# A graph layer on one core: three stages that were programs of their own become one program, with a semaphore where drains stood

## What is computed

```
xn = layernorm(x)
agg = segment_sum(edge_attr, dst) / max(count, 1)           # scatter-add over the edges
h   = relu(concat(xn, agg) @ W1 + b1)                       # 1024 hidden
gnn = xn + h @ W2 + b2
mix = flow_attention(xn) @ W_out.T + b_out                  # sigmoid q and k, per token 8x8 over the heads
x1  = x + gnn + mix
x1n = layernorm(x1)
p   = softmax(mean(x1n, tokens) @ Wg + bg);  e = argmax(p)  # one expert for all tokens
out = x1 + p[e] * (x1n @ We[e] + be[e])
```

## Time and profile before

| | us |
|---|---|
| median of 3 runs | 2229.93 (2226.78 to 2238.92) |
| the profiled execution, its own time | 2234.79 |
| its span, first to last instruction | 2233.1 |
| PE busy in it | 1920.9 |
| mean granted clock of PE | 0.903 of full speed |

### The profile page before, as it was taken

How to read it: one execution, slowest core, us unless ns; L and a number is a source line. 1 busy time by engine, 2 the same in 40 slices (tenths; PEclk the granted TensorE clock), 3 DMA queues, 4 the chain that set the end, 5 groups by cost and what they waited for, 6 DMA issues and landing times. The chain is left out here.

```text
span 2233.1 us, 31150 instructions
## 1 busy us (share of the span) xinstructions
PE 1920.9 (86%) x10775; PEld 1522.4 (68%) x10775; DVE 1222.2 (55%) x3855; ACT 560.4 (25%) x1314; POOL 1341.5 (60%) x876
## 2 busy tenths in 40 slices
PE   2899999999999999688758877777855999998698
PEld 1688887788888788344347766666644888886586
DVE  3534435434344432477565655565536888884575
ACT  2322233322232222111122112111212333332210
POOL 3688888888888888777688878878850000000100
PEclk9899999999999999666867789898777999999799
DMA  9878777787787777887999999999856766652784
GB/s 270 191 154 152 142 139 150 149 153 151 133 160 141 136 142 125 230 206 166 268 228 176 183 189 163 182 202 160 151 98 197 228 207 209 200 180 97 264 303 146
DMA packets 516664, 397.45 MB, mean 178 GB/s; under 512 B 348027, under 2 KB 385163, under 8 KB 516510
## 3 DMA queue, kind: packets, MB, share of 16 engines
q1 hardware_dynamic: 387758, 340.83, 54.5%
q0 software_dynamic: 126640, 54.59, 24.0%
q10 hardware_dynamic: 2112, 0.07, 0.1%
HBM read 242.42 MB, written 152.96 MB: 177 GB/s over the span
## 5 line engine op out<-in xcount | busy, mean ns | idle before, releaser
L286 POOL DMA_INDIRECT table<-edge_sums,edge_row x831 | 1310.8, 1577 | 341.0 <-issue 253.7
L230 DVE SCALAR_TENSOR_TENSOR edge_sel<-edge_dst_all,edge_dst_f,upper 128x128 f32<-128x128 int16 x831 | 316.9, 437 | 105.0 <-PE edge_sum L242 104.8
L338 PE MATMUL pr_out_bank<-pr_norm_xT_hi,pr_w_hi 128*128 128x512 f32 (+1 forms) x832 | 330.1, 397 | 0.0
L338 PE MATMUL pr_out_bank<-pr_norm_xT_lo,pr_w_hi 128*128 128x512 f32 (+1 forms) x832 | 321.1, 386 | 0.0
L338 PE MATMUL pr_out_bank<-pr_norm_xT_hi,pr_w_lo 128*128 128x512 f32 (+1 forms) x832 | 320.9, 386 | 0.0
L242 PEld LDWEIGHTS edge_sum<-edge_attr,edge_sel 128*128 128x128 f32 x1662 | 230.6, 210 | 131.8 <-DVE edge_sel L230 106.5
L242 PE MATMUL edge_sum<-edge_attr,edge_sel 128*128 128x65 f32 x1662 | 244.9, 296 | 80.0 <-DVE edge_sel L230 79.7
L252 ACT ACTIVATE edge_sums<-edge_sum 128x260 f32<-128x260 f32 (+1 forms) x209 | 80.5, 386 | 578.0 <-PE edge_sum L242 546.1
L338 PEld LDWEIGHTS pr_out_bank<-pr_norm_xT_lo,pr_w_hi 128*128 128x128 f32 x832 | 156.8, 188 | 33.8
L338 PEld LDWEIGHTS pr_out_bank<-pr_norm_xT_hi,pr_w_lo 128*128 128x128 f32 x832 | 157.3, 189 | 29.5
L338 PEld LDWEIGHTS pr_out_bank<-pr_norm_xT_hi,pr_w_hi 128*128 128x128 f32 x832 | 157.2, 189 | 28.9
(11 more groups left out here) (202 smaller groups left out, 3254.2 us busy)
## 6 DMA issues: line engine op xcount, KB each, us to landing
edge_dst_all<-dst SPq DMA_DIRECT2D x103, 256.0 KB
edge_attr<-in_edge_attr SPq DMA_DIRECT2D x103, 256.0 KB
qk_T<-pr_stage SPq DMA_DIRECT2D x48, 512.0 KB, 3.3
h_pre_T<-pr_stage SPq DMA_DIRECT2D x48, 512.0 KB, 3.4
gn_pre<-h_pre_T SPq DMA_DIRECT2D x12, 2048.0 KB, 9.6
done<-qk_T SPq DMA_DIRECT2D x16, 1024.0 KB, 6.7
table<-edge_sums,edge_row POOLq DMA_INDIRECT x831
pr_norm_x<-in_x SPq DMA_DIRECT2D x12, 1024.0 KB, 8.6
```

Source lines behind the costliest of these rows:

```text
L230: op = dve.scalar_tensor_tensor(out=self.sel[q][0:rows, j, 0:rows], in0=self.dst_all[k][0:rows, t:t + m * (rows - 1) + 1:m], scalar=self.d ...
L286: pool.indirect_dma_start(self.c.table[t], bass.IndirectOffsetOnAxis(ap=self.row[k][0:rows, j:j + 1], axis=0), self.sums[k][0:rows, j, :], ...
L338: mm = pe.matmul(out, a, c, start=first and i == 0, stop=last and i == n - 1)
```

## The change

- The three programs from projection to expert become one. Their barriers and drains go. Engines go from stage to stage by themselves, held by semaphores.
- POOL: after the last scatter it waits for attention's stores of `base_rows` to land (`over`), then clears the 74 semaphores, waits for the scatters to land, and raises `front_done`. SP, ACT and DVE wait for `front_done` before the MLP's first block. SP no longer waits for the stores.
- SP loads the MLP's weights (2.5 MB, L315) before attention's tail block, behind the last full block's mixing. ACT and DVE split them from there on; DVE splits the W1 part before `front_done`, the two halves of W2 behind it.
- First MLP block: `hid` has four buffers for two; DVE adds two columns ahead of `low`; PE multiplies by W2 column by column as the lo parts come, in place of all after the last. `pre` of block 0, `base` of block 0 and `pre` of block 1 are loaded in that order.
- x1 is kept and stored in quarters of 128 rows, each store waiting for the landing of the one two before it. Before, one store of 512 rows per block.
- Expert: the gate starts on `parts_added`; x1n of block 0 is loaded when the MLP's last full block is through; every chunk of weights has its own semaphore, on which ACT, DVE and PE go; SP waits for the four chunks, not for the bias; the loops over blocks are written out; `out` has two semaphores for its stores, and DVE waits for them itself.

The diff, cut to its core:

```diff
@@ attend_stage
             for batch in batches[2:]:
                 edges.load_ahead(sp, *batch)
+            if b == NB - 1:
+                me.preload(sp)
             sp.wait_ge(acc_free, b * CH + len(subtiles(n)))
...
-        for k in range(2):
-            sp.wait_ge(stored[k], 16 * len(range(k, NB, 2)))
...
+    def over(eng):
+        eng.wait_ge(acc_free, FULL * CH + 1)
+        for k in range(2):
+            eng.wait_ge(stored[k], 16 * len(range(k, NB, 2)))
@@ gnn_stage
+    def preload(sp):
+        sp.wait_ge(before.mixed, FULL * before.STEPS)
+        weights.load(sp)
...
+        sp.wait_ge(c.front_done, 1)
         load_tables(0, BT)
-        weights.load(sp)
         sp.dma_start(b1[:, :], c.b1).then_inc(b1_in, 16)
         load_pre(0, 0, BT)
+        load_base(0, 0, BT)
         load_pre(1, 1, BT)
...
         turn_agg(0, BT)
-        weights.wait(pe)
-        for j in range(JH):
-            hidden(0, 0, BT, j)
-        output(0, 0, BT, 0)
+        weights.wait(pe, 2)
+        for j in range(BANKS):
+            hidden(0, 0, BT, j)
+        for j in range(JH):
+            if j + BANKS < JH:
+                hidden(0, 0, BT, j + BANKS)
+            if j == 0:
+                weights.wait(pe, 4)
+                pe.wait_ge(x1_ready, 1)
+            pe.wait_ge(h_ready, j + 1 + HIDS)
+            mm = products(pe, acc[0][:, :], [(h_hi[0][:, j, 0:P], h_lo[0][:, j, 0:P])],
+                          [(w2_hi[:, j, :], w2_lo[:, j, :])], first=j == 0, last=j == JH - 1)
+        mm.then_inc(acc_mm, 1)
         turn_agg(1, BT)
...
+        def store_x1(b, n, s):
+            r = subtiles(n)[s]
+            pool.wait_ge(x1_ready, b * CH + (AHEAD + s + 1))
+            if b or s >= 2:
+                pool.wait_ge(x1_stored[s % 2], b * 32 + s // 2 * 16)
+            pool.dma_start(c.x1[bass.ds(b * BT + s * P, r), :], x1[s][0:r, :]).then_inc(x1_stored[s % 2], 16)
@@ expert_stage
-            load_xT(0, 0, BT)
-            sp.wait_ge(gathered, 16 * (CH + 1))
+        sp.wait_ge(before.x1nT_stored[0], 16)
+        sp.wait_ge(before.hid_ready, before.AHEAD + FULL * JH)
+        sp.wait_ge(before.x1_ready, before.AHEAD + FULL * CH)
+        load_xT(0, 0, BT)
+        sp.wait_ge(gate_step, 13)
...
+        for ch in range(CH):
+            sp.wait_ge(gathered[ch], 16)
         load_x1(0, 0, BT)
...
         for ch in range(CH):
-            act.wait_ge(gathered, 16 * (CH + 1))
+            act.wait_ge(gathered[ch], 16)
             act.activation(w_hi[:, ch, :], w_raw[:, ch, :], ACT.Copy).then_inc(w_hi_ready, 1)
...
+        dve.wait_ge(before.parts_added, FULL * CH + 2)
@@ kernel_body, gpsimd
             edges.scatter_all(pool)
+            attend.over(pool)
             for sem in project.sems + norms.sems + scale.sems + edges.sems:
                 pool.sem_clear(sem)
             edges.finish_pool(pool)
+            pool.sem_inc(c.front_done, 1)
+            for stage in (gnn, expert):
+                stage.pool(pool)
```

More of the change, by code:

```diff
@@ L1206, in sem @@
         def sem(what):
[L1207 removed]
+            return c.whole.enter_context(nc.semaphore(f"at_{what}"))
         GROUPS = BT // GT
@@ L1211, in attend_stage @@
         HALF = P // 2
-        near = [[sb(f"near0_{half}", [P, 4, P]) for half in range(2)]]
+        near = [[sb(f"near{g}_{half}", [P, 4, P]) for half in range(2)] for g in range(2)]
         q, kk, v, x = [[sb(f"{what}0", shape)] for what, shape in
@@ L1633, in front_stages, with gnn_stage @@
         attend = attend_stage(nc, c, edges, scale)
[L1634 to L1663, removed]
-            edges.finish_pool(pool)
-def gnn_stage(nc, c):
+    return edges, [project, norms, scale, attend]
+def gnn_stage(nc, c, before):
+    me = Shared()
     with ExitStack() as ctx:
@@ new lines, in pe_program, with body @@
+    def pe_program(pe):
+        pe.wait_ge(c.gate_in, 32)
+        pe.wait_ge(gate_step, 1)
+        for ch in range(CH):
+            mm = pe.matmul(small[0:1, 0:EXPERTS], mean[:, ch:ch + 1], c.gate_w[:, ch, :], start=ch == 0,
+                           stop=ch == CH - 1)
+        mm.then_inc(gate_mm, 1)
+        pe.wait_ge(gate_step, 10)
+        pe.matmul(wide[:, 0:2], c.ones_row[:, :], pick[:, :], start=True, stop=True).then_inc(gate_mm, 1)
+        def body(b, k, n, after):
+            pe.wait_ge(xT_ready, b + 1)
+            for s, r in enumerate(subtiles(n)):
+                cut = slice(s * P, s * P + r)
+                if b or s:
+                    pe.wait_ge(y_ready, b * CH + s + 1)
+                for ch in range(CH):
+                    if b == 0 and s == 0:
+                        pe.wait_ge(w_ready, ch + 1)
+                    mm = products(pe, y_bank[s % BANKS][0:r, :], [(xT_hi[k][:, ch, cut], xT_lo[k][:, ch, cut])],
+                                  [(w_hi[:, ch, :], w_lo[:, ch, :])], first=ch == 0, last=ch == CH - 1)
+                mm.then_inc(y_mm, 1)
+        all_blocks(pe, U, body)
@@ new lines, in act_program, with high, ahead @@
+    def act_program(act):
+        def high(b, k, n):
+            act.wait_ge(x_in[k], landed(b, k, U))
+            act.activation(xT_hi[k][:, :, 0:n], xT[k][:, :, 0:n], ACT.Copy).then_inc(xT_hi_ready, 1)
+        act.wait_ge(gate_step, 3)
+        act.activation(prob_e[:, :], logit[:, :], ACT.Exp, bias=neg_top[:, :], accum_out=total[:, :]
+                       ).then_inc(gate_exp, 1)
+        high(0, 0, BT)
+        for ch in range(CH):
+            act.wait_ge(gathered[ch], 16)
+            act.activation(w_hi[:, ch, :], w_raw[:, ch, :], ACT.Copy).then_inc(w_hi_ready, 1)
+        high(1, 1, BT)
+        def ahead(b, k, n, after):
+            if later_size(b, 2):
+                act.wait_ge(y_mm, b * CH)
+                high(b + 2, (k + 2) % U, later_size(b, 2))
+        all_blocks(act, U, ahead)
```

893 lines of the change are left out of this document (446 added, 447 removed).

## The result

| | before | after |
|---|---|---|
| median (range), us | 2233.68 (2226.78 to 2238.92, 4 runs) | 2206.12 (2203.09 to 2208.45, 4 runs) |
| profiled execution, its own time / its span | 2234.79 / 2233.1 | 2203.09 / 2201.3 |

The ratio is 0.9878, 95% interval 0.9854 to 0.9903: 1.2% faster. The fourth run of before was taken beside the new kernel; with it the median of before is 3.75 us above the one that the prediction started from.

What follows compares the result with a forecast made beforehand. The prediction took PE's near-idle time in two junctions, around the MLP, to bound the kernel; 13.8 + 10.1 = 23.9 us less gave 2206.0 us against the median 2229.93, with a range from 2197 to 2215.

Steps and rivals of the forecast that it cites:

- the two junctions: Attention to MLP and MLP to expert stage, where PE stands nearly idle: 13.8 and 10.1 us to be won.
- the gate: Between attention and MLP: drain gone, but clears exposed and tail's store late, so tables are asked for 2.1 us later.
- the two chains: First MLP block, mean to add base, 15.9 us shorter; expert stage's loads, up to DVE's second bias addition, 10.1 us earlier.
- Steady parts gain nothing: MLP's steady part and expert stage: PE is busy throughout at full clock, so nothing can be gained there.
- The store's delay: Tail's store of base_rows, behind the weight loads on its queue: 2.0 us late, bounds 0 and 7.
- Rival 1: Attention to MLP: weights keep the tail's store back by 7 us, scatters suffer too; gain 17, time 2213 us; chance 12%.
- The first block: First MLP block: from the mean to add base 22.6 us in place of 38.5, so 15.9 us won.
- The clock fell at block 1's turn: MLP's second block: up to 2 us less gain if PE's clock falls in its 4 us wait there.
- The second junction: MLP to expert stage: the chain of loads ends last and moves by 10.1 us; PE waits about 4 us.
- The weights' bound: MLP to expert stage: the chain of expert weights alone would allow 14.0 us in place of 10.1.
- Quarter stores: MLP's x1 stores become the bound: each us of landing above 14 costs 2 us in 11 blocks; 2250 at 16; chance 5%.

Runs made afterwards that it cites:

- e4: The kernel before, with only the MLP's buffers allocated in the order of the changed kernel; 2222.13 us in a single run.
- e7: The changed kernel, but in the first MLP block PE multiplies by W2 only behind the last hidden column; 2215.03 us in a single run.
- e10: The changed kernel with the tail's store of base_rows issued as two transfers, of 96 and 10 rows, in place of one of 106; 2198.52 us.
- e5: The changed kernel, but SP loads x1 of block 0 and blocks 1 and 2 without waiting for the four gathers; 2200.65 us in a single run.
- e3: The changed kernel with POOL's clears ahead of its wait for the stores and the MLP's weight loads behind the tail's store; 2197.81 us, ratio to before 0.9857.
- e6: The changed kernel, but ACT splits no expert weights before all four gathers and the bias have landed; 2205.29 us in a single run.
- e12: The kernel before, with only w2_hi and w2_lo allocated behind part, lo ahead of hi; 2230.41 us in a single run.

## Why the prediction was right, point by point

- **The time.** 2206.0 predicted, 2206.12 measured. The mechanism of the two junctions was right, but that the last digit agrees is luck: 3.9 us too little gain (5.0 missed in the MLP, 3.1 too few taken off at the gate, 2.0 more in the two chains than I had), and a median of before that was 3.75 us too low, cancelled.
- **Steady parts gain nothing: the step that failed outright.** I wrote that in the MLP's steady part nothing could be gained because PE is busy for all of it at full clock. I had shown only that nothing makes PE *wait*. The change also moved the buffers, which my list of the change leaves out; two of the three kinds of products became some 2% shorter, and with 0.48 us in each block that is the 5.0 us (e4, with nothing but the buffers moved: 5.4).
- **The gate: right direction, mis-sized.** The clears took 5.6 us behind the store's landing, as said. The store's delay was 5.0, not 2.0: the weights ended 1.8 us later than I had worked out (13.5 us behind the full store's issue, not 11.7), and the tail's store was issued 6.9 us behind the full one in this run, not 8.3. Rival 1 priced this case at 7 us; the truth lies between, inside the bounds. (Its sum of 17 does not follow from that: 23.9 less the 4.9 us between 7 and 2.1 is 19.0; the scatters' share in it has no row.) With another end of attention the term would have come out nearly right: in e7 the tail's store was issued 9.9 us behind the full one and landed in 7.7, 1.1 late. The store's own 4 us at 50 GB/s I took for given, though my text had it on 2 of 16 engines and so how to shorten it: e10.
- **The first block: right.** 22.6 us from the mean to `add base`, 21.8 measured; `low` at 1.3 us a column (1.26), with 0.7 us lost to PE in two of them where I had 1.1; DVE's sum of the next tables ends last. `pre` was in time. The clock fell at block 1's turn, which I had as a bound; that it would fall again in the expert stage I had not.
- **The second junction: right, in place and price.** 10.1 predicted for DVE's second addition, 9.95 measured, and 11.5 to the end (that end moves by 4 us from trace to trace, as shown). PE stood for 4.7 us in blocks 0 and 1 (about 4), 3.4 of them for DVE's bank and 1.3 for weights. e5 shows that the loads bind. Its inner split was wrong: I gave 8.4 to the drain and 1.8 to not waiting for the bias. The program's end gave 8.45 (8.64 to 0.19, token sum to `ex_mean`), and little of that was the drain itself. POOL's own code first waited for its last stores of x1 and x1n to land, until 2064.6, and then drained for 2.2 us (rows below). The bias gave 0.1: from the fourth gather's start to the load of x1 it is 5.29 us after and 5.37 before, since that gather itself takes over 5 us to land there, not 3.6 (in e3 and e6 it was 3.7 and 3.8 to the load). POOL at the end of the MLP, before:

```profile
L1670 POOLq COMPARE_BRANCH  x1: 38/38/38, 2064.6 to 2064.6; - x1
L1670 POOLq DRAIN  x1: 2178/2178/2178, 2064.8 to 2064.8; - x1
```

- **The weights' bound.** I put the other end at 14.0. With the loads free (e5) the junction gives 15.9 to the end and 16.2 to DVE's second addition: the bound was some 2 us too low.
- **Quarter stores: right, from a row misread.** The second of the earlier trace rows counts the expert stage's loads of x1 among the stores; the stores of 512 rows alone landed in 9.2 us in the median and 10.5 at most, not 9.4 and 15.0, which leaves the rival still less room. (Its 2250 at 16 us is 2206 and 2 us x 2 x 11 blocks; the terms 2226 + 24 don't follow from its rule.) Quarters land in 3.7 us in the median, at most in 8.0; POOL waited 35.9 us for them in five times, and PE not at all.

## What to carry to other kernels

When a drain goes, look at what ran under the waits ahead of it: work that was hidden there (here 74 clears, 5.6 us) can move onto the path, and its place in the order is worth as much as the drain (4.8 us). Of two chains that meet, shortening the one that doesn't end last gives little (e6: 1.2 of 6.5 us), and the other one may be held by a wait that no data needs (e5). Look for a stretch of one tenth of the DMA engines at the end of a stage: a transfer with an awkward row count cost 3 to 4 us here, wherever nothing covered it.

## What the runs showed of the hardware that I had not expected

- The time of a product depends on where its operands lie in SBUF: 389 and 390 ns against 395 and 399 for the same 128x512 float32 products, with PE at full clock in both.
- A store of 106 rows (0.2 MB) moves 50 GB/s, and behind 2.5 MB of weights it is seen to move only when these are through: it landed 17.0 to 18.1 us behind their issue in five traces, with its own issue anywhere from 6.5 to 9.5.
- The indirect gathers of the expert weights landed 2.9 us later, as seen by PE's first product, when plain loads of 1 MB each were issued beside them. From issue to landing (least, median, most) in the changed kernel and in e5:

```profile
DMA to landing us min/median/max: 3.5/4.2/5.2
DMA to landing us min/median/max: 6.2/6.4/7.6
```

- GpSimd's drain behind `front_stages` took 4.76 us in three traces (before, e4, e12), though every scatter had landed when it began; the one behind `gnn_stage` took 2.18 in all three.
